# A vision tower on one core: where TensorE does the class-token products of the last attention, and the order of the last group's routing exponentials, gate products and class-token normalisation

## The reference

```python
tokens = (patches @ W.T + b, with the class token in front) * pos_embed
h = tokens
# attention on layernorm(h), 8 heads of 16, softmax over 65 keys
q, k = relu(q), relu(k)
attn = softmax((q @ k.T) / (k.sum(-1) + 1e-6));  h = h + (attn @ v) @ Wo.T + bo
# mixture of experts on a twice normalised h: flat
out_shared = swiglu(flat @ shared_in_w.T) @ shared_out_w.T + shared_out_b
g_idx = argmax(flat @ group_gate_w.T + group_bias)          # 2 groups of 4 experts
e_probs = softmax(expert logits of that group);  top 2, renormalised -> comb
h_expert = swiglu(flat @ expert_in_w.T)                      # one hidden for all experts
routed = sum over e of comb[:, e] * (h_expert @ expert_out_weight[e].T)
h = h + out_shared + routed
```

## Time and profile before

| | before |
|---|---|
| median of 3 runs | 459.95 us (458.52 to 461.21) |
| profiled execution, its own time | 458.25 us |
| its span, first to last instruction | 456.4 us |
| PE, DVE, ACT, POOL busy | 96%, 67%, 42%, 39% of the span |
| mean granted PE clock | 0.994 |

### The profile page before, as it was taken

One profiled execution on the slowest core, in us unless ns is written; L12 is line 12 of the kernel. 1 busy time (PEld: TensorE's weight loads), 2 busy tenths in 40 slices (PEclk: granted clock), 3 DMA queues, 4 the chain that ended last, 5 costly groups with the idle time before them and its releaser, 6 DMA issues.

```text
span 456.4 us, 6968 instructions
## 1 busy us (share of the span) xinstructions
PE 436.9 (96%) x2329; PEld 308.5 (68%) x2329; DVE 307.0 (67%) x895; ACT 190.8 (42%) x362; POOL 178.8 (39%) x217
## 2 busy tenths in 40 slices
PE   6969999899999999999999999999999999999996
PEld 2336455656886677767876588567866778878674
DVE  0152476477766966596848685777678877886686
ACT  1015523753266415742384217632564238522440
POOL 7112721222165316532473127410662254515454
PEclk9999999999999999999999999999999999899999
DMA  8999646134103720074005510360000000010001
GB/s 329 388 405 354 210 158 186 65 116 149 60 1 106 217 70 0 2 250 140 0 1 153 181 55 1 118 201 3 2 13 12 1 1 1 1 25 1 0 2 49
DMA packets 16452, 45.96 MB, mean 101 GB/s; under 512 B 1905, under 2 KB 7585, under 8 KB 16417
## 3 DMA queue, kind: packets, MB, share of 16 engines
q1 hardware_dynamic: 14704, 43.50, 28.2%
q10 hardware_dynamic: 1712, 2.02, 1.3%
HBM read 43.39 MB, written 2.13 MB: 100 GB/s over the span
## 4 chain that ended last, share of the span: by engine, by line
PE 78%; DVE 10%; DMA 4%; issue 4%; POOL 2%; ACTq 1%; ACT 1%; DVEq 0%; POOLq 0%
PE acc L482 22%; PE B L468 5%; PE O L576 5%; DMA bq_row<-in_bq_row 4%; PE scores L702 3%; PE scores L704 3%; PE scores L703 3%; PE C L702 3%; PE scores L546 2%; PE C L704 2%; PE C L703 2%; PE B L525 2%; PE C L634 2%; PE B L511 1%; PE C L635 1%
## 5 line engine op out<-in xcount | busy, mean ns | idle before, releaser
L482 PE MATMUL acc<-x_main,w_patch 128*128 128x512 f32 x288 | 139.4, 607 | 6.0 <-DMA w_patch<-in_w_patch 4.3
L482 PEld LDWEIGHTS acc<-x_main,w_patch 128*128 128x128 f32 x288 | 50.6, 192 | 47.4 <-issue 36.6
L1914 POOL TENSOR_TENSOR prod<-prod 128x512 f32<-128x512 f32 x31 | 39.9, 1287 | 27.6 <-DVE q_nat L1343 10.7
L1002 ACT ACTIVATE probs_t<-B 128x512 f32<-128x512 f32 x32 | 19.0, 595 | 51.5 <-PE B L468 51.5
L576 PEld LDWEIGHTS O<-v_bd,probs_t 128*128 128x128 f32 x256 | 31.9, 192 | 10.4 <-issue 7.6
L1903 POOL TENSOR_TENSOR hidden_lo<-silu,hidden_hi 128x512 fp32r<-128x512 f32 x16 | 20.2, 1268 | 40.8 <-ACT hidden_hi L1002 40.8
L576 PE MATMUL O<-v_bd,probs_t 128*128 128x64 f32 x256 | 31.6, 272 | 0.0
L1845 POOL TENSOR_TENSOR rstd<-var,neg_half 128x4 f32<-128x4 f32 x8 | 8.1, 1017 | 50.8 <-DVE var L1300 50.8
L1002 ACT ACTIVATE probs<-shift 128x512 f32<-128x512 f32 x32 | 20.0, 626 | 18.5 <-DVE shift L1356 16.8
L1002 ACT ACT_TABLE_LOAD x19 | 24.4, 1283 | 7.1 <-issue 6.8
L702 PE MATMUL scores<-w_eout_hi,hidden_hi 128*128 128x512 f32 x64 | 27.3, 426 | 0.0
(11 more groups left out here) (335 smaller groups left out, 1008.0 us busy)
## 6 DMA issues: line engine op xcount, KB each, us to landing
x_main<-in_x_main SPq DMA_DIRECT2D x40, 768.0 KB, 4.4
x_main<-in_x_main SPq DMA_DIRECT2D x8, 512.0 KB, 4.0
x_main<-in_x_main SPq DMA_DIRECT2D x8, 256.0 KB, 3.2
x_tail<-in_x_tail SPq DMA_DIRECT2D x8, 224.0 KB, 4.6
out_tokens<-y_out SPq DMA_DIRECT2D x14, 128.0 KB, 3.1
prod<-in_w_eout SPq DMA_DIRECT2D x2, 512.0 KB, 15.1
w_patch<-in_w_patch ACTq DMA_DIRECT2D x5, 192.0 KB, 10.3
silu<-in_w_in SPq DMA_DIRECT2D x2, 256.0 KB, 13.9
```

The costliest lines, as they stand in the source:

```text
L482: last = mm(acc[:, :], w_patch[:, j, :], x_main[:, j, :], start=(j == 0), stop=False)
L1002: return nc.scalar.activation(dst, src, func, **kw)
L1914: q.tensor_tensor(p[r, 0, :], p[r, 0, :], p[r, 1, :], ALU.add).then_inc(tree1_done.sem, 1)
```

## The change

Four lists change; no instruction is added or removed.

- PE: five of the 32 pairs of `class_values` (11 to 15) go ahead: three between `expert(L - 1, 0)` and `attn_transpose(L)`, two between `shared_natural(L - 1)` and `out_proj(L)`. The other blocks hold 6, 6 and 4 pairs where they held 6, 6 and 9. `ffn_in(L, 3)` goes ahead of `expert(L - 1, 7)` and `class_out`.
- ACT: `route_exp(L)` and the two table loads round it go between the second and third `silus` of L; `counts_out(L)` goes behind the second `hidden_high`.
- DVE: `hidden_mul(L, 3)` goes ahead of `class_residual`; `weigh(L - 1, 7)` ahead of the class tokens' `norm2`; `weights(L)` between that `norm2` and its `norm2_scale`.
- POOL: both `hidden_low(L)` go ahead of the class tokens' `norm_scale2`; `expert_sum(L - 1, 3)` ahead of their `z_low`.

```diff
@@ PE
             expert(L - 1, 0, 128)
+            class_values(EARLY, 14)
             attn_transpose(L)
             shared_natural(L - 1, TILES, 128)
+            class_values(14, 16)
             out_proj(L)
             class_probs(1)
             expert(L - 1, 1, 128)
-            class_values(EARLY, 17)
+            class_values(16, 22)
             expert(L - 1, 2, 128)
-            class_values(17, 23)
+            class_values(22, 28)
             z_transpose(L)
             expert(L - 1, 3, 128)
-            class_values(23, IMAGES // 2)
+            class_values(28, IMAGES // 2)
             ffn_in(L, 0, TOK)
...
             ffn_in(L, 2, TOK)
+            ffn_in(L, 3, TOK)
             expert(L - 1, 7, 128)
             class_out()
-            ffn_in(L, 3, TOK)
             counts(L, TILES, 128)
@@ ACT
             z_out(L, TOK)
-            for k in range(4):
-                silus(L, k, TOK)
-            hidden_high(L, 0, TOK)
-            counts_out(L, TOK)
-            hidden_high(L, 1, TOK)
-            shared_out(L, TOK)
+            silus(L, 0, TOK)
+            silus(L, 1, TOK)
             load_table(L, 3, ACT.Exp)
             route_exp(L, TILES, 128)
+            load_table(L, 4, ACT.Silu)
+            silus(L, 2, TOK)
+            silus(L, 3, TOK)
+            hidden_high(L, 0, TOK)
+            hidden_high(L, 1, TOK)
+            counts_out(L, TOK)
+            shared_out(L, TOK)
             z_out(GROUPS, IMAGES)
-            load_table(L, 4, ACT.Silu)
@@ DVE
             weigh(L - 1, 5, 128)
+            weigh(L - 1, 6, 128)
             hidden_mul(L, 2, TOK)
-            weigh(L - 1, 6, 128)
+            hidden_mul(L, 3, TOK)
             class_residual()
+            weigh(L - 1, 7, 128)
             norm2(GROUPS, h2_cls, 1, IMAGES)
-            hidden_mul(L, 3, TOK)
+            weights(L, TILES, 128)
             norm2_scale(GROUPS, h2_cls, 1, IMAGES)
-            weigh(L - 1, 7, 128)
-            weights(L, TILES, 128)
             weigh(L, 0, 128)
@@ POOL
             expert_sum(L - 1, 2, 128)
-            norm_scale2(GROUPS, 1, IMAGES)
             hidden_low(L, 0, TOK)
             hidden_low(L, 1, TOK)
+            norm_scale2(GROUPS, 1, IMAGES)
+            expert_sum(L - 1, 3, 128)
             z_low(GROUPS, IMAGES)
-            expert_sum(L - 1, 3, 128)
```

## The result

| | before | changed |
|---|---|---|
| median of 20 runs each | 459.97 us | 463.81 us |
| lowest and highest | 457.31, 462.92 | 458.54, 474.30 |
| profiled execution: own time, span | 458.25, 456.4 | 466.99, 465.2 |
| its mean granted PE clock | 0.994 | 0.977 |

The ratio is 1.0048, with a 95% interval of 1.0027 to 1.0068: slower by 0.5%, 2.2 us. The changed kernel's file is a few lines longer, so DVE's and POOL's lines are 4 higher than in the rows of before (L1308 is `norm2_scale`, L1907 `hidden_low`).

The account below looks back on a forecast made before the run. PE, busy 96% of the span, was taken as the bound, with 1.8 us of waits to fill. Net +1.45 us at class_z_transpose and -0.45 behind it gave +1.0 on 459.95: 460.9 us, range 457.9 to 463.0.

Parts of the forecast that it names:

- rival 3: Standstill before class_z_transpose lowers PE's clock: 1.7 us on top, +2.7 in all, 462.65 us; chance 0.15.
- Part 1: Class values in PE's gaps: ffn_in(L, 0) 0.45 us earlier, despite a new wait for z_lo.
- Part 2: Routing exponentials on ACT: third silus ends about 0.3 us later, hidden by other waits; cost 0.
- Part 3: Input products: PE's 0.57 us wait at shared_t(L) goes; expert(L, 0) starts 0.75 us earlier, class-value gain included.
- Part 4: Class tokens' normalisation: POOL holds small DVE ops; PE idles 2.2 us before class_z_transpose, which comes 1.45 later.
- rival 2: Holding is no matter or DVE is early enough, gaps filled as written: 458.9 us, 457.9 at best; chance 0.15.
- Part 5: Behind class_z_transpose: wait at counts(GROUPS) goes and L1549 in the end chain shortens; together -0.45 us.
- The sum: Whole kernel: +1.45 - 0.45 = +1.0 us, giving 460.9 us on 459.95.
- Rivals 1: DVE's small ops get in between POOL's two remainders and POOL is held: sum -0.2, 459.8 us; chance 0.2.

Follow-up runs that it names:

- e4: The kernel before with only the five pairs of class values moved into the gaps; ratio 0.9999 (0.9973 to 1.0024).
- e7: e1 with three pairs of class values in the gaps (two and one) instead of five; median 458.73 us, ratio 0.9960 to the kernel before.
- e5: The changed kernel with the five pairs of class values back in their old blocks; median 463.7 us, ratio 1.0049 to the kernel before.
- the second profile: The changed kernel run once more, unaltered, for another profile; own time 459.49 us, mean clock 0.996.
- e2: The changed kernel with DVE's norm2_scale(GROUPS) ahead of weights(L), POOL's order unaltered; ratio 1.0012 to the kernel before.
- e3: The changed kernel with POOL's z_low(GROUPS) ahead of expert_sum(L - 1, 3), DVE's order unaltered; ratio 0.9978 to the kernel before.
- e6: The changed kernel with nine extra 128x512 matmuls, results unused, in PE's wait before class_z_transpose; median 461.6 us.
- e1: The changed kernel with both norm2_scale(GROUPS) ahead of weights(L) and z_low(GROUPS) ahead of expert_sum(L - 1, 3); ratio 1.0004 to the kernel before.

## Why the prediction was right and where it was off

The forecast was a small loss, +1.0 us within the range 457.9 to 463.0, and the mechanism held: PE stands still for DVE, whose small ops POOL holds. The size came out too small. The ratio gives +2.2 us, just inside "within 0.5%", and inside the range only by the room left for rival 3; the median of all runs, 463.81, lies 0.8 above the range.

- **Part 1**, forecast -0.45: -0.27 (e4 the same). What failed was the 0.1 that I gave back on `out_proj`: it starts 0.44 later, and the wait for z_lo passes on all of it. e7 shows that the size of the block was the matter: three pairs that fit the waits win 0.68, five win 0.27. Both hold against an execution that has the gap; e5 shows one that has none, where five pairs cost 0.45 and three win nothing. The prediction took the gap as always there.
- **Part 2**, forecast 0: the third `silu` ended 0.55 late in the second profile (0.3 reckoned), and no wait on PE points to it. It wasn't tried by itself.
- **Part 3**, forecast -0.75 together with part 1: -0.56. The wait of 0.57 is gone, the new wait for POOL's remainder (0.22) is there as forecast.
- **Part 4**, forecast a standstill of 2.2 us and +1.45: 2.35 us and +1.87. In the second profile, set on the reference matmul, `expert(L, 0)` came 0.2 later than reckoned, but var, the power op and POOL's addition came within 0.05 of the forecast; the rest of the lateness arose in `weights(L)`. That POOL's ops hold small DVE ops was right and is shown by e2 and e3. In detail it went otherwise: two ops got in at the boundary between the remainders, not one, and in `weights(L)` the second op (L1495) was held for 1.77 us instead of L1497 and L1500 of the old numbering for 1.0 and 0.5. It was let go when L1497 was to be, at the end of the addition, but had five more ops behind it, not two, before L1308. The "five rows" set against rival 2 are four in the groups shown: L1304, L1497, L1500 and L1549.
- **Part 5**, forecast -0.45: from +1.87 at L764 to +1.38 at the end, -0.49. L1553, the L1549 of the earlier trace rows, took 0.43 instead of 0.70, and the wait at `counts(GROUPS)` shrank by 0.11.
- **The sum**, forecast +1.0: +1.4 by the second profile. Span times clock says +2.1, the line +2.3. The two prices of part 1 lie 0.7 apart, and the profile of before had a high clock from 396 on; executions without the gap could make the difference, but no run measures it.
- **Rival 3**, the clock, had a chance of 0.15 as a case of its own. It is no case but a share of the runs: behind the standstill the clock was low in two of three profiles, and it cost not the 1.7 us that I took from the earlier trace rows but 4.5 us in the first one. This is the term that was most mis-sized. Filling the standstill brought the median down by 2.2 us (e6), about what the median of all runs has beyond the sum; with 12 runs that is an indication. Rivals 1 and 2 fell in both profiles of the changed kernel.

## What to carry to other kernels

When a step is moved, look at what the neighbour engine does in its new place, not only at what it waits for: in this kernel a VectorE op of 0.14 to 0.33 us took 0.57 to 1.77 us where a GpSimd addition or subtraction of 512 columns held it. Fill a wait with no more than it hides, as the surplus is passed on to the end of the chain, and look in more than one profile whether the wait is always there. And price a new standstill of TensorE at its length plus a chance of a low clock behind it; for that, read the spread of the runs and not only the ratio.

## What the runs showed that I had not expected

A DVE op is held by POOL's *next* op while the power op ahead of it still stands in the record. L1495 started 0.3 us after var's start in the changed kernel and in e3, with the same power op running; with an addition queued behind the power op it took 1.77 us, with none 0.19. So the addition seems to hold the port from before its recorded start; how long before, no run tells, and recorded spans on POOL are rough. The power op itself held no one: L1495 ran through in 0.19 beside it in e3. Nor is it only two-tile ops that are held: L1308, with one tile and two values a partition as inputs, took 1.29 in e2 and 0.34 in e1.

PE gaps depend on the clock upstream: in e5, with the clock low for 8 us before it, the gap that part 1 fills did not exist, and a distance from a reference matmul is a fair measure only between executions with the same waits. And the low clock at 389 lasted from 3 to 10 us in executions of one and the same kernel (the changed one's two profiles), so that a profile of one execution can be 3 us off its kernel's median for no reason of the change.
